# A DLRM tower on one core: gathers, transposes and grams in quads of four tiles

## The reference

```python
e = jnp.stack([tbl_0[ids[:, 0]], ..., tbl_31[ids[:, 31]]], axis=1)      # (512, 32, 256)
dots = jnp.einsum('bnd,bmd->bnm', e, e)
z = dots[:, iu, ju]                                                     # i < j: (512, 496)
h = jnp.concatenate([z, dense_ctx], axis=1)                             # (512, 512)
h = jnp.maximum(h @ W_top1 + b_top1, 0.0)                               # 512 -> 512
h = jnp.maximum(h @ W_top2 + b_top2, 0.0)                               # 512 -> 256
y = h @ W_top3                                                          # 256 -> 1
```

## Time and profile before

| | |
|---|---|
| time, median of 3 runs | 251.21 us (251.07 to 251.59) |
| the profiled execution: span | 251.4 us |
| PE busy, matmuls | 166.6 us (66%), 2544 |
| PEld, weight loads | 113.4 us (45%), 2544 |
| POOL | 121.6 us (48%) |
| DVE, ACT | 69.8 us (28%), 57.1 us (23%) |
| bytes moved by DMA | 18.91 MB, of it 16.79 MB gathers |
| mean granted clock of TensorE | 0.756 |

### The profile page before, as it was taken

One profiled execution on the slowest core, in us unless ns is written; L12 is line 12 of the kernel. 1 busy time (PEld: TensorE's weight loads), 2 busy tenths in 40 slices (PEclk: granted clock), 3 DMA queues, 4 the chain that ended last, 5 costly groups with the idle time before them and its releaser, 6 DMA issues.

```text
span 251.4 us, 6104 instructions
## 1 busy us (share of the span) xinstructions
PE 166.6 (66%) x2544; PEld 113.4 (45%) x2544; DVE 69.8 (28%) x253; ACT 57.1 (23%) x193; POOL 121.6 (48%) x132
## 2 busy tenths in 40 slices
PE   0431076666667994766667995666665974779976
PEld 0211043333335962433335973333333952447765
DVE  0000014151515025151515015151515014244331
ACT  2000003131313113131313113131313123134231
POOL 4777365556566155656666146666565235600000
PEclk9999999999999996555555597555555596555989
DMA  5833223222322112322322112222222112200000
GB/s 138 286 105 106 76 70 94 83 80 85 87 85 83 38 51 80 92 82 83 85 81 82 42 42 83 83 83 83 81 83 89 44 42 85 86 23 3 4 0 0
DMA packets 7766, 18.91 MB, mean 75 GB/s; under 512 B 2593, under 2 KB 3489, under 8 KB 7618
## 3 DMA queue, kind: packets, MB, share of 16 engines
q0 software_dynamic: 6144, 16.79, 22.9%
q1 hardware_dynamic: 1602, 1.84, 2.4%
HBM read 18.62 MB, written 0.00 MB: 74 GB/s over the span
## 4 chain that ended last, share of the span: by engine, by line
PE 63%; DVE 18%; another core or an unknown queue 7%; issue 6%; DMA 3%; ACT 2%; POOL 0%; DVEq 0%; ACTq 0%
PE xt_ps L274 28%; PE gram_ps L287 19%; PE mlp_ps L306 9%; DVE z L183 9%; DVE xt L175 7%; PE mlp_ps L317 4%; PE mlp_ps L297 2%; DMA rows<-in_table,row_number 2%; DVE slots L193 1%; ACT xt L175 1%; ACT slots L238 1%; DMA ids_sb<-in_ids 1%; POOL rows L165 0%; PE mlp_ps L325 0%
## 5 line engine op out<-in xcount | busy, mean ns | idle before, releaser
L165 POOL DMA_INDIRECT rows<-in_table,row_number x128 | 121.4, 948 | 98.6 <-PE xt_ps L274 68.1
L287 PE MATMUL gram_ps<-xt 128*32 128x32 f32 x2048 | 57.6, 238 | 68.1 <-DVE xt L175 50.6
L287 PEld LDWEIGHTS gram_ps<-xt 128*32 128x32 f32 x2048 | 40.7, 142 | 110.2 <-DVE xt L175 59.8
L274 PE MATMUL xt_ps<-identity,rows 128*128 128x128 f32 x256 | 81.9, 418 | 12.8 <-DMA rows<-in_table,row_number 9.8
L175 DVE COPY xt<-xt_ps 128x256 f32<-128x256 f32 x64 | 27.2, 425 | 156.7 <-PE xt_ps L274 136.8
L175 ACT COPY xt<-xt_ps 128x256 f32<-128x256 f32 x64 | 23.9, 373 | 121.1 <-PE xt_ps L274 89.2
L274 PEld LDWEIGHTS xt_ps<-identity,rows 128*128 128x128 f32 x256 | 35.6, 191 | 21.4 <-issue 12.8
L183 DVE COPY z<-slots 32x32 f32<-32x32 f32 x160 | 34.2, 214 | 2.5
L183 ACT COPY z<-slots 32x32 f32<-32x32 f32 x96 | 23.4, 244 | 4.3 <-DVE slots L193 2.9
L306 PE MATMUL mlp_ps<-z,w1z_sb 128*128 128x128 f32 x128 | 23.1, 364 | 1.9 <-DVE z L183 1.9
L306 PEld LDWEIGHTS mlp_ps<-z,w1z_sb 128*128 128x128 f32 x128 | 22.4, 276 | 2.7 <-issue 2.7
(11 more groups left out here) (6 smaller groups left out, 1.8 us busy)
## 6 DMA issues: line engine op xcount, KB each, us to landing
rows<-in_table,row_number POOLq DMA_INDIRECT x128
w1z_sb<-in_w1z SPq DMA_DIRECT2D x1, 1024.0 KB, 5.0
w_sb<-in_w SPq DMA_DIRECT2D x1, 512.0 KB
ids_sb<-in_ids SPq DMA_DIRECT2D x1, 64.5 KB, 1.8
identity<-in_eye SPq DMA_DIRECT2D x1, 64.0 KB, 1.9
upper_sb<-in_takes_upper SPq DMA_DIRECT2D x1, 64.0 KB, 1.9
ctx_sb<-in_ctx_t SPq DMA_DIRECT2D x1, 32.0 KB
w1c_sb<-in_w1c SPq DMA_DIRECT2D x1, 32.0 KB
```

The costliest lines, as they stand in the source:

```text
L165: nc.gpsimd.indirect_dma_start(rows[:, n % SLOTS, :], None, table, bass.IndirectOffsetOnAxis(ap=row_number[:, n:n + 1], axis=0),).then_inc ...
L274: last = nc.tensor.transpose(xt_ps[g % 2][:, k, :], rows[:, g % SLOTS, k * P:(k + 1) * P], identity[:])
L287: last = nc.tensor.matmul(gram_ps[u % 2][F * j:F * j + F, g % UNIT, :], x, x, start=(k == 0), stop=(k == KD - 1))
```

## The change

- `rows` holds 16 pairs of tiles (32 tiles). POOL waits at every second gather, for the pair that held the slots.
- PE works in quads of four tiles: two pairs are transposed (8 transposes), then both pairs of the quad before get their grams. Semaphores tell of pairs, no longer of tiles.
- `xt_ps` is four full PSUM banks of a pair each; a pair waits for the copy of the pair four before it. `xt` holds 12 pairs. A copy is of a pair, 512 elements a partition: DVE the even pairs, ACT the odd ones.
- `z` has room for all 512 samples. The layers run over five batches: 32, 32, 32, 16 and 16 tiles (128 or 64 columns), at quads 9, 17, 25 and 29 (`TURN`), layer 2 one quad later, layer 3 two; the last one behind the last grams, with `h1` in four PSUM banks of its own, and layer 2 between the parts of layer 1.
- DVE spreads 9 cells of a unit and ACT 7. `take_lower` also waits until both engines have spread the unit two before.
- Nothing is a loop any more; all four engines' programs are written out.

```diff
-SLOTS = 16
-XT_SLOTS = 8
+RING = 16
+XT_RING = 12
+BATCHES = [(0, 4), (4, 4), (8, 4), (12, 2), (14, 2)]
+TURN = [2 * (first + units) + 1 for first, units in BATCHES]
-DVE_CELLS, ACT_CELLS = CELLS[:10], CELLS[10:]
+DVE_CELLS, ACT_CELLS = CELLS[:9], CELLS[9:]
-        rows = sbuf("rows", [P, SLOTS, D])
+        rows = sbuf("rows", [P, RING, 2, D])
-        xt = sbuf("xt", [P, XT_SLOTS, KD, P])
+        xt = sbuf("xt", [P, XT_RING, 2, KD, P])
-        z = sbuf("z", [P, MM, N])
+        z = sbuf("z", [P, MM, B])
-        xt_ps = [psum(f"xt_ps{i}", [P, 2 * KD, P])[:, 0:KD, :] for i in range(2)]
+        xt_ps = [psum(f"xt_ps{i}", [P, 2, KD, P]) for i in range(4)]
...
-            for n in range(B // J):
-                if n >= SLOTS:
-                    pool.wait_ge(rows_transposed, n + 1 - SLOTS)
+            for n in range(TILES):
+                p = n // 2
+                if p >= RING and n % 2 == 0:
+                    pool.wait_ge(transposed, p - RING + 1)
                 nc.gpsimd.indirect_dma_start(
-                    rows[:, n % SLOTS, :], None, table,
+                    rows[:, p % RING, n % 2, :], None, table,
...
+        def copy_pair(engine, copy, p):
+            if p >= XT_RING:
+                engine.wait_ge(gram_ready, p - XT_RING + 1)
+            engine.wait_ge(transposed, p + 1)
+            copy(xt[:, p % XT_RING], xt_ps[p % 4][:]).then_inc(xt_ready[p % 2], 1)
...
+            for quad in range(QUADS):
+                copy_pair(dve, nc.vector.tensor_copy, 2 * quad)
+                if quad and quad % 2 == 0:
+                    take_upper(quad // 2 - 1)
+                    spread(dve, nc.vector.tensor_copy, DVE_CELLS, z_dve, quad // 2 - 1)
...
+            def take_lower(u):
+                act.wait_ge(gram_ready, (UNIT // 2) * (u + 1))
+                if u >= 2:
+                    act.wait_ge(z_dve, u - 1)
+                    act.wait_ge(z_act, u - 1)
...
+            def transposes(p):
+                if p >= 4:
+                    pe.wait_ge(xt_ready[p % 2], (p - 4) // 2 + 1)
+                pe.wait_ge(rows_landed[p % RING], 32 * (p // RING + 1))
+                for i in range(2):
+                    for k in range(KD):
+                        last = nc.tensor.transpose(xt_ps[p % 4][:, i, k, :], rows[:, p % RING, i, k * P:(k + 1) * P],
+                                                   identity[:])
+                last.then_inc(transposed, 1)
...
+            for quad in range(QUADS):
+                last_quad = quad == QUADS - 1
+                transposes(2 * quad)
+                if not last_quad:
+                    transposes(2 * quad + 1)
+                if quad:
+                    gram(2 * quad - 2)
+                    gram(2 * quad - 1)
+                for batch in range(LAST):
+                    if quad == TURN[batch]:
+                        context(batch)
+                        z_complete(batch)
+                        for n in range(KH1):
+                            if n >= 2:
+                                pe.wait_ge(h1_ready, batch * KH1 + (n - 1))
+                            layer1(batch, n)
+                    if quad == TURN[batch] + 1:
+                        pe.wait_ge(h1_ready, batch * KH1 + KH1)
+                        for n in range(KH2):
+                            layer2(batch, n, range(KH1))
+                    if quad == TURN[batch] + 2:
+                        layer3(batch)
+                if last_quad:
+                    gram(2 * quad)
+                    transposes(2 * quad + 1)
+            gram(PAIRS - 1)
+            context(LAST)
+            z_complete(LAST)
+            layer1(LAST, 0)
+            for k in range(KH1):
+                if k + 1 < KH1:
+                    layer1(LAST, k + 1)
+                for n in range(KH2):
+                    layer2(LAST, n, [k])
+            layer3(LAST)
```

More of the change, by code:

```diff
@@ L54, with samples, count @@
 TAKES_UPPER = np.where(LANE < S, LANE >= SLOT, LANE - S < SLOT)
[L59 to L69, removed]
+def samples(batch):
+    first, units = BATCHES[batch]
+    return slice(first * UNIT * J, (first + units) * UNIT * J)
+def count(batch):
+    return BATCHES[batch][1] * UNIT * J
 def dlrm_tower(nc, table, ids, eye, takes_upper, ctx_t, w1z, w1c, b1, w2, b2, w3, y):
@@ L262, in _ @@
-            quarters(nc.scalar, quarter)
-            take_lower(NQ - 1, UNITS - 1)
-            spread(act, nc.scalar.copy, ACT_CELLS, z_act, NQ - 1, UNITS - 1)
-            relu1(NQ - 1)
+                for n in range(KH1):
+                    act.wait_ge(h1_done, batch * KH1 + (n + 1))
+                    nc.scalar.activation(h1_sb[:, n, 0:count(batch)], h1_ps(batch, n), ACT.Relu,
+                                         bias=b1_sb[:, n:n + 1]).then_inc(h1_ready, 1)
+            for quad in range(QUADS):
+                copy_pair(act, nc.scalar.copy, 2 * quad + 1)
+                if quad and quad % 2 == 0:
+                    take_lower(quad // 2 - 1)
+                    spread(act, nc.scalar.copy, ACT_CELLS, z_act, quad // 2 - 1)
+                for batch in range(LAST):
+                    if quad == TURN[batch]:
+                        relu1(batch)
@@ L267, in _ @@
+            take_lower(UNITS - 1)
+            spread(act, nc.scalar.copy, ACT_CELLS, z_act, UNITS - 1)
+            relu1(LAST)
         @block.tensor
         def _(pe):
-            def transposes(t, g, first):
-                if not first or g >= 2:
-                    pe.wait_ge(xt_ready[g % 2], t * (G // 2) + g // 2)
-                pe.wait_ge(rows_landed[g % SLOTS], t * (G // SLOTS * 16) + (g // SLOTS + 1) * 16)
-                for k in range(KD):
-                    last = nc.tensor.transpose(xt_ps[g % 2][:, k, :], rows[:, g % SLOTS, k * P:(k + 1) * P],
-                                               identity[:])
-                last.then_inc(rows_transposed, 1)
@@ new lines, in gram @@
+            def gram(p):
+                u = 2 * p // UNIT
+                pe.wait_ge(xt_ready[p % 2], p // 2 + 1)
+                if (2 * p) % UNIT == 0 and u >= 2:
+                    pe.wait_ge(slots_ready, u - 1)
+                for i in range(2):
+                    g = (2 * p + i) % UNIT
+                    for j in range(J):
+                        for k in range(KD):
+                            x = xt[:, p % XT_RING, i, k, F * j:F * j + F]
+                            last = nc.tensor.matmul(gram_ps[u % 2][F * j:F * j + F, g, :], x, x, start=(k == 0),
+                                                    stop=(k == KD - 1))
@@ L321, in layer3, with z_complete @@
-            def layer3(t):
+                    own_bank = batch == LAST or n < 2
+                    nc.tensor.matmul(h1_ps(batch, n), w1c_sb[:, n * P:(n + 1) * P], ctx_sb[:, samples(batch)],
+                                     start=own_bank, stop=False, skip_group_check=True)
+            def z_complete(batch):
+                first, units = BATCHES[batch]
+                pe.wait_ge(w1_loaded, 16)
+                pe.wait_ge(z_dve, first + units)
+                pe.wait_ge(z_act, first + units)
```

190 lines of the change are left out of this document (65 added, 125 removed).

## The result

The changed kernel takes 274.22 us (median of 4 runs, 273.62 to 275.3) against 251.14 us for the kernel before in the same comparison: a ratio of 1.093, with a 95% interval of 1.089 to 1.097. The forecast was 261. The sign was right and the time lies inside the range of 236 to 288, but the loss is 23 us where 10 were forecast.

A forecast was written before the change was run, and what follows sets the result against it. Bound: engines waiting in a ring, PE's completions reaching others late while POOL issues gathers. Sum: 56 (start) + 140 (coupled gathers) + 11 (layers inside) + 43 (after the last gather) + 10.9 (end) = 261 us; range 236 to 288.

The forecast's parts named there:

- layers inside: Layer batches 0 and 1 while gathers still run: POOL stands still 5.6 us at each, as before, 11 us.
- the coupled rate: Time per gather while POOL and PE wait for each other: 1.59 us, between 1.405 and 1.96; 88 gathers cost 140 us.
- the first hold: Delay of PE's completions after the 40 gathers at the start: 4.0 us, so first release at 56 us.
- the end: Last layers after the last grams: 12.9 us before, 2 less through half the columns, so 10.9 us.
- The last stretch: PE's work after the last gather: 33 tiles at 1.01 us, plus batches 2 and 3, minus 7 us; 43 us together.
- last gather: POOL done with its gathers at 56 + 140 + 11 = 207 us, where it was 220 before.
- signs named ahead: Copy gap until about 56 us, 40 gathers unpaused, later fours with pauses, last near 207, PE stopped by issue mid-grams.
- The limit of 66 open records: PE stops at 66 unanswered records; a pair's 72 just fit, a quad's 144 do not, leaving 78 after the hold.
- A: Rival: PE's quad fits under four gathers, 1.405 us each, 16 us less, 245; decided below 1.47; chance 0.20.
- B: Rival: late copies come from something else, such as too few PSUM buffers; POOL's pace alone binds, about 180 us; chance 0.10.
- C: Rival: PE's remainder of a quad lies open in full, 1.96 us a gather, 33 us more, 294; over 280 has chance 0.15.

The follow-up runs named there:

- the interleaved version: Changed kernel with PE's order in a quad made transposes, grams, transposes, grams: 256.47 us, ratio 1.026, where the kernel before takes 250.39 us.
- the plain loads: Changed kernel with POOL issuing plain DMAs of 128 consecutive rows instead of indirect gathers, gather by ids left out: 133.61 us where the kernel before takes 250.39.
- single tiles and a short ring: Kernel before with 8 tiles of rows in flight instead of 16 (SLOTS = 8): 244.07 us, ratio 0.973, where the kernel before takes 250.79 us.
- free condition: Jobs in which the kernel before takes about 197 us and no late PE completions are in the trace; changed kernel unchanged there: 186.61 us, ratio 0.941.
- held condition: Jobs in which the kernel before takes about 251 us and PE's completions come late while POOL issues gathers; changed kernel unchanged there: 274.76 us, ratio 1.097.
- SyncE's loads: Changed kernel with row loads issued by SyncE as plain DMAs, gather by ids left out: 128.42, 130.11 and 125.54 us where the kernel before takes about 197.

## Why the prediction was right in sign and small in size

The mechanism that was forecast, late completions under POOL's gathers, is in the trace. What failed is the size: a loss of 23 us where 10 were forecast. The term that was most short is **layers inside**, put at 11 us "as before" and measured at 18, because POOL waits at a turn for the held grams of a whole quad as well as for the layers. Three more terms were short: the coupled rate (+5), the first hold (+3) and the end (+4). The last stretch was 8 us better than its term and hid part of this, which is luck. Step by step, with the terms of the sum:

| term | forecast | measured | difference |
|---|---|---|---|
| 40 gathers at the start, then the first release | 56 | 59.1 | +3 |
| 88 gathers in the coupled stretch | 88 x 1.59 = 140 | 88 x 1.65 = 145 | +5 |
| layers inside, two turns | 11 | 163 - 145 = 18 | +7 |
| last gather | 207 | 222 | +15 |
| from there to the last grams | 43 | 34.6 | -8 |
| the end | 10.9 | 15.2 | +4 |
| time above the span of the profiled run | 0 | 274.2 - 271.8 = 2.4 | +2 |
| sum | 261 | 274.2 | +13 |

- **Time and span.** In most of the runs the time stands 1.8 to 2.2 us above the span. The trace of the kernel before, with a span of 251.4, is therefore of an execution some 2 us longer than the median of 251.21, and not of the median's length as I had taken it.
- **"While POOL issues gathers, PE's completions reach the others late"** held. Of the signs named ahead, four were in the trace: the gap after the first copies (to 58.84, forecast about 56), 40 gathers without a pause, four in a row afterwards, and a stop by "issue" in the middle of the grams. The last gather came 15 us later than forecast, and the tiles of the last stretch cost well under 1.01 us. That the lump of a quad's grams between the releases costs most of the loss is shown by the interleaved version (18 of 24 us back); that the indirect gathers are behind the hold, by the plain loads (133.61 us). Four gathers in a row are not dear by themselves: the short steps of four cost 1.54 a gather, as two at a time do.
- **The first hold** was taken as the 4.0 us of 20 gathers. With 40 it was 6.6. I had written that a longer run holds longer, and then did not use it. From POOL's last start to its next one there are 2.65 us after 12 gathers, 4.62 after 16, 4.22 after 20 and 6.86 after 40: longer on the whole, not step by step.
- **The coupled rate** of 1.59 stood between bounds of 1.405 and 1.96, and 1.65 is well inside, but as a mean of short and long steps. That five of the six long ones come with a unit's spread is something that no term of the sum had in it. With the lump halved the rate is 1.54, with single tiles and a short ring 1.52.
- **"Layers inside … POOL stands still for 5.6 us at each, as before"** is the term that added most. POOL is released by transposes, and in the new order a turn stands behind a whole quad's grams, which are themselves held (until 110.5 in the turn shown), with the layers of 5.6 and 2.1 us behind them and layer 2 behind the next quad's grams as well. The price was not POOL's pause of before but the length of the work that stands between two releases, twice. The 18 is a remainder of the sum. The two turns, read at their gaps, give about 9 and 11.
- **The limit of 66 open records** is neither shown nor refuted. 41 matmuls with 41 loads went out in one burst at 15.98, and 46 matmuls at 78.33. Either part of them had been completed by then, or the limit counts in another way. The order of the size is all that the traces bear out.
- **The last stretch** was the other way. I had given the faster clock to ten tiles after each turn. In the trace it stayed from the turn of batch 2 (231 us) to the last grams, and a tile cost 0.45 us, less than the 0.65 of the earlier trace rows. At the 1.2 GHz level, too, a tile cost 0.75 us and not the 1.01 of the earlier trace rows. So "the deeper PSUM ring finds nothing to shorten in this stretch" does not hold for the change as a whole: it saves 0.2 us a tile at the faster clock and 0.26 at the slower one, and no run separates the order from the buffers.
- **The end** was forecast shorter by 2 us and came out longer: 15.2 against 12.9 us. Half the columns save nothing: at a granted clock of 1.00 layer 1 took 3.84 us with 128 columns (230.99) and 3.79 with 64 (245.11), with as many weight loads in both. In the end itself it took 6.9 us, more than the 5.44 of the earlier trace rows. What the end lost beside the forecast goes with the clock: 0.54 in 259 to 271 us, after PE had waited for DVE ahead of its layers, where the window of the kernel before over its last layer 1 (241.4 to 247 us) shows 0.70.
- **The rivals.** A (four gathers pay, 245) is out: 1.65 is above its 1.47. C (the remainder in full, 294) is out on the same number. B (PE is not held) had 0.10 and is what happens in the free condition, for this kernel and for every version of it. There the change does what its size suggests, since POOL's 160 us of issue bind and nothing interrupts them.
- **The short ring.** That a shorter ring helps in the held condition is shown for the kernel before (7 us), and is false for the changed one (4 us worse with 8 tiles; 16 tiles ran in a free job alone). My account of the second case (more waiting turns and a shorter dense tail) is read from one trace and not separated.

**What stays open** is what puts a job into one condition or the other. It was the same for all runs of a job, it differed between jobs some minutes apart, and chip, time and placement in memory were not separated. Nor was it tried whether SyncE's loads are also free of the hold, since they ran in free jobs alone. How an indirect gather delays PE's completions is not in any trace, nor whether PE does its work late or only reports it late: the traces show that most completions arrive when the gathers pause. It does not hit all engines alike: DVE's copy of the earlier trace rows is over at 69.46, and PE starts the grams that wait for it at 69.52, in the middle of a gather (69.21 to 70.15). That PE's instructions reach it late while gathers run would also give the records in ones and twos behind "issue"; it would not explain a copy that starts 18 us after its last transpose has left (40.41 to 58.84).

## What to carry to other kernels

When a copy starts long after the transposes it waits for should be over, suspect late completions and look at what POOL issues in that time; then look at how much PE work lies between two releases of POOL, and spread the releases: two tiles of grams between them cost 18 us less than four. Loads that need no indices should not be indirect ones: the same bytes by plain loads, without the gather by ids, took the kernel from 274 to 134 us in the held condition and from 187 to 130 in the free one. And measure the kernel before again on another chip and at another time before trusting a ratio: this change was 1.09 and 0.94 of it.

## What the runs showed of the hardware that I had not expected

- One kernel, 251 or 197 us, by the job. The difference is the hold of PE's completions during indirect gathers, and its 54 us are more than any edit changed that keeps the gathers.
- While gathers run without a pause in the held condition, PE still gets one or two matmuls out every 0.7 us at first, and mostly one every 1.4 to 2.8 us from 30 us on.
- An indirect gather of 128 rows of 1 KB occupies POOL 0.95 us and comes every 1.25 us in both conditions. A plain load of the same size occupies it 0.54 us.
- In a burst PE issues 41 to 48 gram matmuls, with as many weight loads, before it stops behind "issue". The Trainium skill states a queue depth of 64 for TensorE ("TensorE: Matmul & The Clock Gate", the table ahead of its first section). The bursts of 82 to 96 records fit that only if a part of them had completed, which no run here shows.
